# The decay to the chunk's end moves from the corrections to the keys: one multiplication leaves VectorE, another joins GpSimd

## The reference

```python
def step(S, inp):
    q_t, k_t, v_t, b_g, b_beta = inp
    S = S * jnp.exp(b_g)[..., None, None]
    kv = jnp.einsum('mbhk,mbhkv->mbhv', k_t, S)
    dv = (v_t[None] - kv) * b_beta[..., None]
    S = S + k_t[..., :, None] * dv[..., None, :]
    o_t = jnp.einsum('mbhk,mbhkv->mbhv', q_t, S)
    return (S, o_t)
```

## Time and profile before

| | us |
|---|---|
| time, median of 3 runs (lowest, highest) | 7000.74 (6998.04, 7004.32) |
| the profiled execution's own time | 6999.14 |
| its span, first to last instruction | 6997.4 |
| busy VectorE, TensorE, ScalarE, GpSimd | 5135.8, 4452.0, 3430.8, 2767.8 |
| one loop iteration (two halves), from 3020.53 to 3213.18 | 192.65 |
| mean granted TensorE clock, of full speed | 0.817 |

### The profile page before, as it was taken

The page is one execution under the profiler, slowest core; times in us unless marked ns, Lnnn a source line. Parts: engine busy times, 40 slices in busy tenths (PEclk is TensorE's granted clock), DMA queues, the critical chain, the costliest instruction groups (busy, mean ns, idle before and its releaser), DMA issues. The chain is left out here.

```text
span 6997.4 us, 195918 instructions
## 1 busy us (share of the span) xinstructions
PE 4452.0 (64%) x78513; PEld 3830.1 (55%) x78513; DVE 5135.8 (73%) x9800; ACT 3430.8 (49%) x6010; POOL 2767.8 (40%) x1789
## 2 busy tenths in 40 slices
PE   1666666666666666666666666666666666655993
PEld 1555555555555555555565555555555655553662
DVE  4888778888887887878888888778888888881003
ACT  1555555555555555555555555555555555542220
POOL 3444343444343443434443434434344443434003
PEclk6878878888887788888888787887878887887997
DMA  2000000000000000000000000000000000002223
GB/s 88 2 5 5 6 5 5 5 5 3 4 5 5 5 5 6 5 5 5 5 3 5 5 5 5 5 6 5 5 5 5 3 5 5 5 27 95 72 72 105
DMA packets 77479, 109.71 MB, mean 16 GB/s; under 512 B 20576, under 2 KB 66208, under 8 KB 75424
## 3 DMA queue, kind: packets, MB, share of 16 engines
q1 hardware_dynamic: 67616, 71.42, 3.2%
q0 software_dynamic: 8960, 25.39, 1.2%
HBM read 57.89 MB, written 38.89 MB: 14 GB/s over the span
## 5 line engine op out<-in xcount | busy, mean ns | idle before, releaser
L1573 POOL TENSOR_TENSOR state<-state,gc_end 128x512 f32<-128x512 f32 x512 | 591.5, 1172 | 1852.4 <-PE bank L595 1811.9
L589 PE MATMUL bank<-rhs,te 128*64 128x64 f32 x8192 | 412.6, 254 | 765.9 <-DVE rhs L1291 490.0
L572 PE MATMUL bank<-state,ke 128*64 128x64 f32 x16384 | 656.1, 248 | 341.0 <-DVE outT L1309 221.4
L572 PEld LDWEIGHTS bank<-state,ke 128*64 128x64 f32 x16384 | 616.8, 160 | 415.8 <-DVE state L1307 237.1
L797 ACT ACTIVATE te<-tt 32x256 f32<-32x256 f32 x1024 | 421.9, 412 | 802.6 <-DVE tt L1275 792.0
L589 PEld LDWEIGHTS bank<-rhs,te 128*64 128x64 f32 x8192 | 345.0, 163 | 844.4 <-DVE rhs L1291 795.8
L608 PE MATMUL last_two<-dvs,kte 128*64 128x64 f32 x16384 | 658.9, 241 | 180.1 <-DVE dvs L1298 180.1
L1272 DVE TENSOR_TENSOR last_two<-last_two,prod 128x31 f32<-128x31 f32 (+15 forms) x1984 | 692.4, 349 | 68.2
L847 ACT ACTIVATE ke<-kq 32x512 f32<-32x512 f32 x1024 | 642.9, 628 | 201.7 <-DVE kq L1223 188.0
L1270 DVE TENSOR_TENSOR prod<-bd,last_two 128x31 f32<-128x31 f32 (+15 forms) x1984 | 671.1, 338 | 68.3
L608 PEld LDWEIGHTS last_two<-dvs,kte 128*64 128x64 f32 x16384 | 597.2, 154 | 196.5 <-DVE dvs L1298 187.3
(11 more groups left out here) (257 smaller groups left out, 10221.1 us busy)
## 6 DMA issues: line engine op xcount, KB each, us to landing
w_sb<-in_L_ffn_W_dram SPq DMA_DIRECT2D x16, 1024.0 KB, 9.5
expert_rows<-ke SPq DMA_DIRECT2D x1, 8192.0 KB, 21.9
xrows<-expert_rows SPq DMA_DIRECT2D x16, 512.0 KB, 8.4
expert_outputs<-yrow POOLq DMA_DIRECT2D x16, 512.0 KB, 3.4
xt<-_attn_hidden_states_dram SPq DMA_DIRECT2D x32, 128.0 KB, 2.9
xr<-_attn_hidden_states_dram SPq DMA_DIRECT2D x32, 128.0 KB, 2.1
x_after_attention<-xr SPq DMA_DIRECT2D x32, 128.0 KB, 1.7
xo<-x_after_attention SPq DMA_DIRECT2D x32, 128.0 KB, 3.9
```

What stands on the lines that cost most here:

```text
L572: mm = pe.matmul(bank_mem[g][s, q % 4 * DK:q % 4 * DK + DK], ke[:, c, r, q, s], state[:, hh * HQ + q, r, :], start=(r == 0), stop=(r == 1))
L589: pe.matmul(bank_mem[g][s, q % 4 * DK:q % 4 * DK + DK], te[:, q, s], rhs[:, q, :], start=True, stop=True)
L1573: pool.tensor_tensor(sv, sv, gc_end[:, vh, 4 * g:4 * g + 4, c].unsqueeze(2).broadcast_to([P, 4, 2 * DK]), ALU.mult).then_inc(sem(f"state_f ...
```

## The change

dec_end, the decay from a token to the end of its chunk, depends on the token, the quad and the chunk. It used to multiply the corrections (by VectorE, in each chunk and group, into dvs). Now GpSimd multiplies the turned keys kt by it, in place, once a half for all four chunks (`fade_keys`, after pw). The update then uses ScalarE's copy dv, as the outputs do, and dvs is gone. `take_dv` waits for TensorE's dv_full instead of VectorE's dvs; the first `expand_kte` of a half waits for kt_faded instead of kt_ready; ScalarE signals dec_end_ready. Besides, the last stage loads xo with one transfer for four tiles instead of four.

```diff
@@ update_and_outputs (TensorE)
                 for g in range(2):
-                    pe.wait_ge(sem(f"dvs_ready{g}"), since(f"dvs_ready{g}", vc + 1))
+                    pe.wait_ge(sem(f"dv_ready{g}"), since(f"dv_ready{g}", vc + 1))
                     pe.wait_ge(sem("kte_ready"), vc + 1)
...
-                                               kte[:, r, q, s], dvs[:, q, :], start=True, stop=True)
+                                               kte[:, r, q, s], dv[:, q, :], start=True, stop=True)
                     mm.then_inc(sem(f"upd_full{g}"), 1)
-                    pe.wait_ge(sem(f"dv_ready{g}"), since(f"dv_ready{g}", vc + 1))
                     pe.wait_ge(sem("pw_ready"), since("pw_ready", v + 1))
@@ take_dv, half (ScalarE)
-                    act.wait_ge(sem(f"dvs_ready{g}"), since(f"dvs_ready{g}", 4 * v + c + 1))
+                    act.wait_ge(sem(f"dv_full{g}"), 4 * v + c + 1)
...
-                act.activation(dec_end[:, hh], dec[:, :, :, C - 1], ACT.Copy)
+                act.activation(dec_end[:, hh], dec[:, :, :, C - 1], ACT.Copy).then_inc(sem("dec_end_ready"), 1)
...
-                act.wait_ge(sem("kt_ready"), u + 1)
+                act.wait_ge(sem("kt_faded"), u + 1)
                 expand_kte(u, 0)
@@ VectorE
-            def decayed_corrections(v, hh, c):
-                vc = 4 * v + c
-                for g in range(2):
-                    of = slice(4 * g, 4 * g + 4)
-                    dve.wait_ge(sem(f"dv_full{g}"), vc + 1)
-                    vec(dve.tensor_tensor(dvs[:, of], bank_mem[g][:, 0:4 * DK].rearrange("p (q v) -> p q v", q=4),
-                                          dec_end[:, hh, of, c].unsqueeze(2).broadcast_to([P, 4, DK]), ALU.mult), f"dvs_ready{g}", vc + 1)
...
-                memories(decayed_corrections, 0)
-                memories(decayed_corrections, 1)
-                memories(decayed_corrections, 2)
-                memories(decayed_corrections, 3)
...
-                decayed_corrections(2 * NT - 1, 1, c)
@@ GpSimd
+            def fade_keys(u, hh):
+
+                pool.wait_ge(sem("kt_ready"), u + 1)
+                pool.wait_ge(sem("dec_end_ready"), u + 1)
+                by = dec_end[:, hh].unsqueeze(3).broadcast_to([P, HQ, NC, FR])
+                for r in range(2):
+                    kv = kt[:, r].rearrange("p q (c f) -> p q c f", c=NC)
+                    ins = pool.tensor_tensor(kv, kv, by, ALU.mult)
+                ins.then_inc(sem("kt_faded"), 1)
...
                 vec(pool.tensor_tensor(pw[:], pw[:], w_quad[:, q0:q0 + HQ].unsqueeze(1).unsqueeze(3).broadcast_to([P, NC, HQ, C]), ALU.mult), "pw_ready", u + 1)
+                fade_keys(u, hh)
                 if not last:
                     low_turns(*after(n, hh), general=first)
@@ last stage (SyncE, VectorE)
-                    for g in range(G):
-                        sp.dma_start(xo[:, b, g], x1_dram[bass.ds((i * 2 * G + b * G + g) * P, P), :]).then_inc(sem(f"xo_in{b}{g}"), 16)
+                    sp.dma_start(xo[:, b], x1_dram[bass.ds((i * 2 * G + b * G) * P, G * P), :].rearrange("(g p) d -> p g d", p=P)).then_inc(sem(f"xo_in{b}"), 16)
...
-                        dve.wait_ge(sem(f"xo_in{b}{g}"), 16 * (i + 1))
+                        dve.wait_ge(sem(f"xo_in{b}"), 16 * (i + 1))
```

## The result

| | before | after |
|---|---|---|
| time, median of 4 runs (lowest, highest), us | 7002.53 (6998.04, 7007.15) | 7145.37 (7138.29, 7149.59) |
| ratio, 95% interval | | 1.0203 (1.0185 to 1.0221) |
| profiled execution, its own time and its span | 6999.14, 6997.4 | 7143.56, 7141.9 |

What follows compares the result with a forecast made beforehand. VectorE is busiest, but GpSimd's squares stand in a slackless chain to the logits: 122.5 us there, 3 us more in even halves and 22.5 in odd ones make 148 us, 7149 us; range 7075 to 7185.

Steps and rivals of the forecast that it cites:

- rival (a): The forecast: logits' wait grows 3.95 us, freed VectorE time lost to port lock and ScalarE; 7149 us, chance 0.72.
- Chunk 0: State update in a half's first chunk: 0.7 us sooner in even halves, 0 saved in odd ones.
- GpSimd's products: fade_keys, two products between pw and low_turns in GpSimd's list: 3.95 us a half.
- The logits' wait: VectorE's wait for the router's logits in even halves: 3.95 us longer, near 10.9 us, some 340 us in all.
- rival (b): Lock doesn't follow VectorE's next operation, so chunk 0 gives 1.5 and 1.1 us; 7091 us, chance 0.14.
- a state update of chunk 0 a full microsecond sooner: Sign in chunk 0 that, if seen, would make the prediction wrong in part.
- Chunk 1: Update now hangs on ScalarE's copy dv: TensorE starts 1.07 us later, 0.8 us lost in every half.
- Chunks 2 and 3: 0 saved: L1223 about 3.2 us but ending no sooner; wait before the first chunk system near 1.8 us.
- The load of xo: Last stage, one 512 KB load instead of four: some 3 us more once an iteration, VectorE catches up; 0, at most 4 us.
- Rival (c): VectorE's removed time of chunks 0 and 1 comes off whole, 168 us; 6955 us, chance 0.07.
- (d): Something between the forecast and 6955 us that lands within 0.2% of no change; chance 0.03.
- (e): GpSimd's new product is dearer, like 3.2 us for one held up: 78 us more, 7227 us, chance 0.04.

Runs made afterwards that it cites:

- e1: Kernel after with fade_keys moved behind high_turns and group_rows, at the end of GpSimd's list: 7049.9 us, ratio 1.0053.
- e2: Kernel before with fade_keys added on GpSimd and VectorE's dvs product kept, multiplying by ones: 7062.2 us, ratio 1.0079.
- e7: Kernel after without GpSimd's fade of the state in each half's first chunk, only semaphores raised: 7109.0 us, ratio 1.0153.
- e4: Kernel after with ScalarE's copy of chunk 1's corrections ahead of the cosine instead of behind it: 7072.0 us, ratio 1.0092.
- e3: Kernel after without GpSimd's two new products, keys left undecayed and only the semaphore raised: 7037.6 us, ratio 1.0046.
- e5: Kernel after with the router's part ahead of the sum of squares on TensorE and ScalarE: 6888.3 us, ratio 0.9837.
- e9: Kernel before with the router's part ahead of the sum of squares: 6879.2 us, ratio 0.9822.
- e11: Kernel after with router ahead of squares, chunk 1's copy ahead of the cosine, and fade_keys at the end of GpSimd's list: 6840.7 us, ratio 0.9768.

## Why the prediction was right

The time, the sign and the place were as forecast: rival (a), with its mechanism in the wait for the logits and in chunk 1. Chunk 0 was mis-sized, and that the even half came out within 0.03 us is luck, as the terms show:

- **GpSimd's products.** Forecast 3.95 us a half, measured 3.74 from start to start. e1 and e2 show from both sides that they act by standing ahead of the squares: without that place the even half is 3.45 us shorter, with it alone 4.14 longer.
- **The logits' wait.** Forecast 340 us in all, measured 336.7. The wait grew in the loop by 4.15: the 3.74, and 0.41 us that I had not foreseen, by which the sums of squares take longer on average (the clock, below). The two errors cancel.
- **Chunk 0.** Forecast 0.7 us sooner in an even half and 0 in an odd one (0.1 in the sum); measured 1.27 and 0.25 on average. In the half shown first it is 0.88: there L1171 and L1172 stretched as the sum had it. But the sum took it that the fade always comes first. It starts together with L1171, and in 16 of 31 even halves L1171 wasn't held up, so that the update came 1.7 us sooner than before, more than the 1.5 of rival (b). The recorded sign "a state update of chunk 0 a full microsecond sooner" thus came true, and this term is wrong in part; it is worth some 18 us in even halves and 5 in odd ones. What hid it there: the 0.35 us of VectorE's wait after the last outT, which no term had, and the 0.2 us by which the wait for the logits grew more than the 3.95. e7 shows that GpSimd's fades stretch L1171 and L1172. Without these fades chunk 0 is 1.62 us (even) and 1.25 (odd) shorter than before, and chunk 1 gives back 0.15 and 0.12 of it: 1.47 and 1.13, close to the 1.5 and 1.1 us of rival (b). e7 took only 36 us off the kernel after, where (b) lies 58 below the forecast, because the kernel after had part of that gain already.
- **Chunk 1.** Forecast 0.8 us lost, measured 0.80 (even) and 0.76 (odd), with TensorE's start 1.05 us later (1.07 forecast). e4 shows the cause by taking it away.
- **Chunks 2 and 3.** L1221 takes 3.20 us (3.2 forecast) and the state update waits 1.04 us behind it, as before. The wait for the first chunk system was forecast at 1.8 us and is 2.19 in the row below, so nothing was saved there.

```profile
3131.54 0.42 DVE L1254 TENSOR_TENSOR cos_t<-bank,bd 128x256 f32<-128x256 f32 x1 [2.19 <-PE bank L532]
```

- **Sum by halves.** Even halves +4.05 forecast, +4.02 measured (4.15 - 1.27 + 0.80 + 0.35). Odd +0.7 forecast, +0.48 measured. There the terms of the chunks come to +0.51, so the delay did cost nothing; but that held only by an accident of phase. The new products move GpSimd's list against VectorE's clip and scan: e2 alone makes odd halves 2.04 us shorter, and e3 alone 0.88 longer. The two sum to -1.16; together the halves are 0.48 longer, and 1.17 us of the 1.64 between are the clip, which takes 1.54 us where e2's takes 0.37. In the kernel after the clip is 0.91 us longer than before and the scan 1.09 shorter, and the two all but cancel. The forecast of the odd halves was near, and its reason incomplete.
- **The load of xo.** Forecast 0, at most 4 us. VectorE waits longer for it; in the length of the stage the traces show 0.7 us, which is within their spread.

Rival (c) falls by e3, (d) and (e) by the result.

## What to carry to other kernels

Work taken from the busiest engine is worth only what is last behind it: here e3 gave back 217 us of VectorE's work and lost 31. In chunk 1 the consumer had to turn to a copy that another engine makes behind an activation, which took about as much as chunk 0 gave. Before work is put into another engine's list, look for what stands behind it there and who waits for that; the chain from the squares to the router held up both kernels, and cutting it took 257 us off the kernel after (e5) and 124 off the kernel before (e9). When a change is a loss, try it again with the thing removed that eats it: with the router first and the copy early, this one gains 68 us. And a step is measured by all its repetitions: in the half shown first, chunk 0 is 0.4 us off the mean of 31.

## What the runs showed of the hardware

**The shared port, in small instructions.** In this kernel a TENSOR_SCALAR of 64x128 f32 took 0.28 us at the seam of two of GpSimd's products (e2) and 1.97 beside one of them (after). The scan of 64x128 took 0.49 on average in e2 and 1.65 before. The Trainium skill, SBUF — State Buffer, section Who interferes with whom, says that the two engines share a pair of ports as an exclusive lock, and that the second to issue is blocked until the first is through. L1221's 3.20 us and the clip agree. How long it lasts changes with the phase: in e2, where GpSimd's list from the low turns on starts some 3.7 us later, the clip and the scan of an odd half took 1.42 us less with no less work. The clip of e2 got in between two products that GpSimd runs without a gap, so there the waiting side was served next.

**A tie at the port.** In chunk 0 of the even halves L1171 and the first fade start within 0.03 us of each other. In 16 of 31 halves L1171 took 1.2 us and the two fades 3.6 together; in 15 L1171 took 2.1 us and the first fade 1.05. The update came 0.8 us sooner in the former. What decides is open; with the new products elsewhere in GpSimd's list (e1, e11) it was the fade in all 31.

**TensorE's clock behind a longer wait.** In the kernel before the two sums of squares took 2.07 us in 15 of the 31 even halves of the loop, 1.12 to 1.48 in 15 and 1.87 in one, 1.67 on average. The windows below (us of the stretch, busy time of TensorE, weight load, VectorE, ScalarE, GpSimd with counts, granted clock, DMA share, GB/s) are of the kernel before, around the sums and the logits in two even halves:

```profile
2895.20:2907.70 12.50, 3.99 (x18) 2.37 (x16) 5.98 (x17) 7.97 (x15) 11.01 (x6) 0.74 0.07 22
3089.00:3101.50 12.50, 3.90 (x10) 1.72 (x8) 5.14 (x14) 7.89 (x14) 10.09 (x6) 0.63 0.07 21
```

In the first the two sums took 1.24 us, and the wait for the logits is 6.09 us, shorter by 0.86 than the 6.95 of the earlier trace rows; 0.83 of it are the sums. The clock granted during the sums alone was 0.85 there and 0.50 in the second. In the 3.8 us ahead of them, in which TensorE ran no matmul, it was 1.00 in the first and 0.90 in the second. The kernel after, with 7.78 us of idle TensorE ahead of the sums in place of 4.04:

```profile
3155.00:3170.00 15.00, 3.78 (x8) 1.72 (x8) 4.00 (x11) 6.90 (x14) 11.95 (x7) 0.56 0.07 19
```

Here the granted clock was 0.50, the lower of the two levels (1.2 GHz), from 3157.0 on and over the sums. They take 2.07 or 2.08 us in all 31 even halves, 0.41 more than the mean before, which is what the wait for the logits grew by beyond GpSimd's 3.74. That the longer idle time is what leaves the clock at the lower level is likely and not shown: in e1, with the shorter idle time again, 28 of the 31 waits for the logits are 6.9 to 7.0 us as well.
